# Routing a mixture of experts in two parts: the first 48 token tiles inside the attention stage, the last 16 behind it

## The reference, cut to what matters

```python
x = x + ga * attention(layernorm(x) * (1 + ca) + sa)
h = layernorm(x) * (1 + cb) + sb
logits = einsum('bsh,eh->bse', h, router_w)           # 8 experts
probs = softmax(logits)
weights, indices = top_k(probs, 2)
weights = weights / (weights.sum(-1, keepdims=True) + 1e-06)
gate, up = split(einsum('bsh,ehi->bsei', h, w13))      # 2 x 512 per expert
y = einsum('bsei,eih->bseh', silu(gate) * up, w2)
x = x + gb * (take(y, indices) * weights[..., None]).sum(2)
```

## Time and profile before

| what | us |
|---|---|
| median of 3 runs | 1350.82 |
| the three runs | 1350.82, 1351.5, 1343.63 |
| time of the profiled execution | 1345.89 |
| its span in the trace | 1344.1 |
| last logits copied by ACT | 677.96 |
| first instruction of the experts block | 678.23 |
| first gather on POOL | 723.14 |

### The profile page before, as it was taken

The page is one execution under the profiler, slowest core; times in us unless marked ns, Lnnn a source line. Parts: engine busy times, 40 slices in busy tenths (PEclk is TensorE's granted clock), DMA queues, the critical chain, the costliest instruction groups (busy, mean ns, idle before and its releaser), DMA issues. The chain is left out here.

```text
span 1344.1 us, 54731 instructions
## 1 busy us (share of the span) xinstructions
PE 1188.2 (88%) x20142; PEld 1014.1 (75%) x20142; DVE 939.0 (70%) x2509; ACT 706.3 (53%) x1391; POOL 929.5 (69%) x989
## 2 busy tenths in 40 slices
PE   3589999999899899998616899999999999999995
PEld 0377878778777777777405799999999999999994
DVE  2389999999999999988477555555555555555552
ACT  3277888888888888887531223322232223222221
POOL 3158999999999889998803466666666666666643
PEclk8599999999999999999555999999999999999998
DMA  9811333334333333343372354545454555555540
GB/s 232 173 54 49 84 97 91 88 102 119 106 102 115 96 111 105 104 116 108 92 201 72 72 96 94 98 93 96 90 97 94 96 97 98 98 99 97 97 70 1
DMA packets 126348, 134.52 MB, mean 100 GB/s; under 512 B 26298, under 2 KB 104210, under 8 KB 125970
## 3 DMA queue, kind: packets, MB, share of 16 engines
q0 software_dynamic: 32592, 56.75, 21.9%
q1 hardware_dynamic: 89762, 67.46, 18.8%
q10 hardware_dynamic: 3744, 6.82, 1.8%
HBM read 63.58 MB, written 44.04 MB: 80 GB/s over the span
## 5 line engine op out<-in xcount | busy, mean ns | idle before, releaser
L1143 PE MATMUL psum<-xT,xall 128*128 128x256 f16 x3408 | 397.2, 274 | 1.5 <-DVE xT L1130 0.9
L1203 POOL DMA_INDIRECT out<-yo,sidx x142 | 226.5, 1595 | 198.9 <-DVE yo L1194 175.3
L1143 PEld LDWEIGHTS psum<-xT,xall 128*128 x3408 | 331.6, 98 | 40.0 <-issue 1.9
L1151 ACT ACTIVATE sg<-psum 128x512 f32<-128x512 f32 x142 | 84.7, 597 | 318.7 <-PE psum L1143 304.6
L1156 DVE SCALAR_TENSOR_TENSOR hf<-psum,sg 128x512 f32<-128x512 f32 x142 | 98.3, 692 | 214.4 <-ACT sg L1151 208.3
L1113 POOL DMA_INDIRECT grow<-moe_rows,gidx x142 | 144.4, 1017 | 93.7 <-DVE sidx L1001 50.8
L1177 PE MATMUL psum<-w2s,hT 128*128 x1704 | 199.3, 274 | 3.8 <-DVE w2s L1229 3.5
L1177 PEld LDWEIGHTS psum<-w2s,hT 128*128 128x128 f16 x1704 | 167.4, 98 | 24.4 <-issue 4.3
L1163 ACT ACTIVATE hT<-hf 128x512 f16<-128x512 f32 x142 | 89.4, 630 | 112.7 <-DVE hf L1156 100.6
L569 POOL TENSOR_TENSOR pT<-sc,pT 128x1024 f16<-128x1024 f32 x64 | 136.7, 2135 | 9.8 <-ACT pT L565 9.8
L1167 DVE TENSOR_TENSOR hT<-hf,hT 128x512 f16<-128x512 f32 x142 | 98.4, 693 | 57.0 <-ACT hT L1163 49.4
(11 more groups left out here) (217 smaller groups left out, 2414.1 us busy)
## 6 DMA issues: line engine op xcount, KB each, us to landing
stk<-qk SPq DMA_DIRECT2D x384, 64.0 KB, 2.8
moe_rows<-hrows SPq DMA_DIRECT2D x128, 128.0 KB, 2.7
out<-xall SPq DMA_DIRECT2D x128, 64.0 KB, 2.4
xall<-in_x SPq DMA_DIRECT2D x8, 896.0 KB, 17.6
raw<-in_w ACTq DMA_DIRECT2D x26, 256.0 KB, 3.2
raw<-in_w SPq DMA_DIRECT2D x8, 512.0 KB, 8.8
grow<-moe_rows,gidx POOLq DMA_INDIRECT x142
out<-yo,sidx POOLq DMA_INDIRECT x142
```

Of the source, the lines that this page charges most:

```text
L1143: i = k.e.matmul(bank[:, n * LONG:(n + 1) * LONG], w13s[:, bass.ds(ex_reg * (G * 4 * I) + ((2 * c + b_) * 2 * I + col), P)], xT[:, k.b, a, ...
L1151: done(k.e.activation(sg[:, half, :], bGate[half][:, :], ACT.Silu, scale=1.0 / W_SCALE), "sg")
L1203: k.e.indirect_dma_start(out_rows, bass.IndirectOffsetOnAxis(ap=sidx[:, n:n + 1], axis=0), yo[:, k.v, q, :], None, bounds_check=B * T - 1, ...
```

## The change

The chain over 64 tiles becomes a class `Part` with methods for its steps, made twice: `early` for tiles 0 to 47 (384 elements in a partition) and `late` for tiles 48 to 63 (128 elements).

- Early on DVE, in rounds 73 to 76: the choice of the best two, 12 instructions and the one that makes `chosen`, behind `ln2_shift` (`choice_a`), `resid` (`choice_b`) and `var_eps2` (`choice_c`). Behind DVE's rounds, still in the attention block: `early_rest`, with the weights, the count and the places.
- Early on ACT: two Exp behind `logit_copy` of round 75. On PE: two prefix matmuls behind `router` of round 71 into banks B and C.
- Early on SP: behind its last `store`, 8 transfers with the weights of 12 of the 16 segments, and behind the waits for the stores a wait for these 8 to have landed.
- In the experts block the chain runs over 16 tiles; one subtraction more takes the counts of the early part into account, and `tile_0` is made by two instructions. Eight transfers write the remaining weights. From `rsel` on all is as before.
- The early scratch lies in buffers of the attention that are free by then (`ex`, `rel`, `sig`, `qk`), what the late part needs in `wqkv`, which now lives through both blocks. `hf` and `yo` of the slots lie on `late13`.

```diff
+EARLY = 48
+N_EARLY = E * EARLY
+ROUND_CHOICE, ROUND_PREFIX, ROUND_EXP = 73, 71, 75
...
+    def gaps2(self, e, s_gap):
+        e.tensor_tensor(self.e2, self.m2, self.m1, ALU.subtract).then_inc(s_gap, 1)
+        self.link(e, e.tensor_tensor(self.gap2, self.gap2, bc_mid(self.m2, E), ALU.subtract))
...
+        start = upto[:, :, 0]
+        if self.t0:
+            self.link(e, e.tensor_tensor(self.start, start, self.placed.cnt, ALU.subtract))
...
+    def choice_a(e, i):
+
+        if i == ROUND_CHOICE:
+            e.wait_ge(S["lg"], EARLY)
+            early.largest(e)
+            early.gaps(e, e_gap)
+        if i == ROUND_CHOICE + 1:
+            early.one_hot(e, early.oh1, early.r1)
+        if i == ROUND_CHOICE + 2:
+            early.gaps2(e, e_gap)
+        if i == ROUND_CHOICE + 3:
+            early.one_hot(e, early.oh2, early.r2)
+            early.choose(e, e_chosen)
+    def choice_b(e, i):
+
+        if i == ROUND_CHOICE + 1:
+            early.without_first(e)
+        if i == ROUND_CHOICE + 2:
+            early.hits(e, early.gap2)
+    def choice_c(e, i):
+
+        raw_low(e, i)
+        if i == ROUND_CHOICE:
+            early.hits(e, early.gap)
+            early.first_of(e, early.r1)
+        if i == ROUND_CHOICE + 1:
+            early.second(e)
+        if i == ROUND_CHOICE + 2:
+            early.first_of(e, early.r2)
...
+        if i == ROUND_EXP:
+            e.wait_ge(e_gap, 2)
+            e.activation(early.ex, early.gap, ACT.Exp).then_inc(e_exp, 1)
+            e.activation(early.e2, early.e2, ACT.Exp).then_inc(e_exp, 1)
+    def early_prefix(e, i):
+        if i == ROUND_PREFIX:
+            e.wait_ge(S["umul"], NT)
+            e.wait_ge(e_chosen, 1)
+            for q, bank in enumerate((bkB, bkC)):
+                e.matmul(bank[:, 0:N_EARLY], trib[:, q, :], chosen.bitcast(BF16), start=True, stop=True).then_inc(e_prefix, 1)
+    def early_rest(e):
+        e.memset(one, 1.0)
+        e.memset(early.seen[:, 0:1], 0.0)
+        early.weights(e, e_exp, e_chosen, e_placed)
+        e.wait_ge(e_prefix, 2)
+        early.count(e, one, by_expert(bkB[:, 0:N_EARLY]), bkC[:, 0:N_EARLY], placed.cnt)
+        early.place(e, e_placed)
+    chunk_work = {p_high: raw_load, logit_copy: early_exp, ln2_shift: choice_a, resid: choice_b, var_eps2: choice_c,
+                  router: early_prefix}
...
             engine_program("sync", e)
+            e.wait_ge(e_placed, 1)
+            weights_out(e, rows_dram, early.w8, 0, EARLY // NJ, e_w8)
             for j in range(4):
                 e.wait_ge(s_st[j], 32 * NS)
             for j in range(4):
                 e.wait_ge(s_out[j], 32 * NS)
+            e.wait_ge(e_w8, 16 * B)
...
             engine_program("vector", e)
+            early_rest(e)
```

More of the change, by code:

```diff
@@ L49 @@
 OOB = B * T + 4096
+NGATHER, NADD = 6, 4
 NCH, NEARLY, NRAW = E * G, 13, 3
@@ L80, in adaln_block @@
         passed = sem("passed")
+        s_g, s_sc = [sem(f"f_row{i}") for i in range(NGATHER)], [sem(f"f_add{i}") for i in range(NADD)]
         idf = sb("idf", [P, P])
@@ L814, in raw_low, with taken, by_expert @@
             w13_low(e, w13s, raw[:, n % NRAW, :], n).then_inc(s_rlo, 1)
-    chunk_work = {p_high: raw_load, logit_copy: raw_high, var_eps2: raw_low}
+    e_v, e_gap, e_exp, e_chosen = sem("e_v"), sem("e_gap"), sem("e_exp"), sem("e_chosen")
+    e_prefix, e_placed, e_w8 = sem("e_prefix"), sem("e_placed"), sem("e_w8")
+    def taken(home, *sizes):
+        at = [sum(sizes[:i]) for i in range(len(sizes) + 1)]
+        return [home[:, a:b] for a, b in zip(at, at[1:])]
+    def by_expert(ap):
+        return ap.rearrange("p (e t) -> p e t", e=E)
@@ new lines, in attention @@
+    NE = N_EARLY
+    gap, gap2, m1, m2, e2, z, g = taken(ex[:, :, :].rearrange("p b n -> p (b n)"), NE, NE, *([EARLY] * 5))
+    expd, seen, one, oh1 = taken(rel[:, :, :].rearrange("p b n -> p (b n)"), NE, NE + 1, 1, NE // 2)
+    where, w8, hit = taken(sig[:, :, :, :, :, :].rearrange("p k a g b t -> p (k a g b t)"), NE, NE, NE // 2)
+    oh2, chosen, over, row_at, r1, r2, row32 = taken(qk[:, :, :, :, :].rearrange("p b w a n -> p (b w a n)"), NE, NE, NE, NE,
+                                                     EARLY, EARLY, 4 * EARLY)
@@ new lines, in attention @@
+    early = Part(0, EARLY, dict(
+        gap=by_expert(gap), gap2=by_expert(gap2), m1=m1, m2=m2, e2=e2, z=z, g=g, ex=by_expert(expd), seen=seen,
+        oh1=by_expert(oh1.bitcast(F16)), where=by_expert(where), w8=w8.rearrange("p (t e) -> p t e", e=E),
+        hit=by_expert(hit.bitcast(F16)), oh2=by_expert(oh2), chosen=by_expert(chosen.bitcast(BF16)), over=by_expert(over),
+        row_at=by_expert(row_at), r1=r1, r2=r2, row32=row32.bitcast(F32).rearrange("p (t q) -> p t q", q=2)),
+        placed, placed.lt0, logits, iota, tok_id, e_v)
@@ L906, in route_sync @@
         e.wait_ge(s_weights, 1)
[L907 to L912, removed]
+        weights_out(e, rows_dram, w8, EARLY // NJ, NS, s_w8)
     def route_vector(e):
         def link(ins):
[L915 to L920, removed]
+            late.link(e, ins)
         e.memset(one[:, :], 1.0)
@@ L971, in route_vector @@
-        link(e.tensor_copy(row_of[:, :, :], row32[:, :, :]))
+        late.largest(e)
+        late.gaps(e, s_gap)
+        late.hits(e, late.gap)
+        late.first_of(e, late.r1)
+        late.one_hot(e, late.oh1, late.r1)
+        late.without_first(e)
+        late.second(e)
+        late.gaps2(e, s_gap)
+        late.hits(e, late.gap2)
+        late.first_of(e, late.r2)
+        late.one_hot(e, late.oh2, late.r2)
+        late.choose(e, s_chosen)
+        late.weights(e, s_exp, s_chosen, s_weights)
@@ L972, in route_vector @@
+        e.wait_ge(s_prefix, 2)
+        late.count(e, one, bBefore[:, 0:E * NL].rearrange("p (e t) -> p e t", e=E), bTotal[:, 0:E * NL], cnt[:, :])
+        late.place(e, s_asel)
         groups = 2 * NT // NHOT
-        rows = row_of[:, :, :].rearrange("p t q -> p (t q)")
+        rows = row_of.rearrange("p t q -> p (t q)")
         for k in range(groups):
@@ L1016, in route_scalar @@
         e.wait_ge(s_gap, 2)
[L1017 to L1018 removed]
+        e.activation(late.ex, late.gap, ACT.Exp).then_inc(s_exp, 1)
+        e.activation(late.e2, late.e2, ACT.Exp).then_inc(s_exp, 1)
         e.wait_ge(s_2, 16 * E)
```

182 lines of the change are left out of this document (108 added, 74 removed).

## The result

| | before | after |
|---|---|---|
| median of 17 runs each, us | 1348.53 | 1354.33 |
| lowest to highest | 1342.91 to 1353.36 | 1347.93 to 1360.36 |
| span of the profiled execution | 1344.1 | 1358.2 |

The account below looks back on a forecast made before the run. PE bounds attention and slots; the routing between is serial, so the first gather's shift decides. The block ends 6.8 us later, tile_no and gather 5.3: 1351.2 on the profiled execution, 1356.1 on the median, middle 1354; range 1347 to 1361.

Parts of the forecast that it names:

- path B: Loads of w2 after the experts block's start, eight ACT conversions, then tile_no: tile_no and first gather 5.3 us later.
- signs by which the forecast was to be wrong: Block end before 680 or after 690, tile_no waiting for DVE as before, or slots not taking 621 us.
- Step 1: DVE's late chain from z to first rsel: 15.25 us becomes 8.1, removing 7.2 us of this path.
- Step 2: DVE's choice instructions in rounds 73 to 76: all that follows comes 1.05 us later, bounds 0 and 7.2.
- Step 3: Exp on ACT and prefix matmuls on PE: 0.35 and 0.2 us on the last logits, covered by later steps.
- Step 4: DVE's early_rest behind its rounds: 12.8 us, ending at 683.2; alone it delays the attention block's end by 5.0.
- Step 5: SP's eight early weight writes and their landing end the attention block at 685.0, 6.8 us later than before.
- R1: Writes cost less, early_rest sets the block's end (+5.0), gather moves 3.5 us: 1349.4; chance 0.20.
- Step 6: Sum at the first gather: first rsel 0.4 us earlier, but tile_no and the gather 5.3 us later.
- R2: Each of 13 choice instructions delays its round, itself or through POOL: up to 7.2 us, 1357.3; chance 0.15.
- R3: Early part vanishes beside the last tiles, block ends as before; gain held to 1.5 us, 1344.4; chance 0.08.
- R4: Late chain isn't shortened because small instructions cost as much as large ones: +6.8, 1352.7; chance 0.02.

Follow-up runs that it names:

- after_tile_first: Changed kernel with ACT's eight w2 conversions moved behind tile_no and the two table copies; ln2_shift of tile 59 to first gather 77.5 us, ratio to before 0.9997.
- after_padded: Changed kernel with early f16 scratch hit at 64 elements per expert (stride 128 bytes, not 96); ln2_shift to first gather 83.6 us, one execution, no ratio.
- after_choice_behind: Changed kernel with all 13 choice instructions moved from DVE's rounds to the head of early_rest, Exp and prefix behind the rounds; ln2_shift to first gather 90.8 us.
- after_no_w8_wait: Changed kernel with the wait for the eight early weight writes moved from SP to POOL's first gather; ln2_shift to first gather 84.7 us, ratio to before 1.0082.
- split_tile_first: Changed kernel with early places in the experts block, early writes behind w2 loads, tile_no before w2 conversions; ln2_shift to first gather 72.0 us, ratio to before 0.9967.
- split: split_tile_first with tile_no back behind ACT's w2 conversions; ln2_shift of tile 59 to first gather 79.9 us, ratio to before 1.0024.

## Why the prediction was right, step by step

The forecast was 5.3 us more, and 1354 us. The mechanism on which it hangs was right: path B, the loads of w2 behind the block's end and the conversions ahead of tile_no, which after_tile_first shows. That the median came within 0.3 us of 1354 is luck in two ways. The middle between a quick execution and the median of three was chosen for want of a better one, and 17 runs put the median of before just there (1348.53). And the block's end came out near its forecast although another engine set it: a landing put too long was made up for by DVE's instructions, which were put too short in steps 2 and 4.

Two of the signs by which the forecast was to be wrong need a word. The block ended at 690.5, past the named 690, but this trace runs 4.55 us late before the change begins; on the scale of the kernel before it ended at 686.0. And the slots took 623.9 us in this trace for the 621 named; that is the part left open below.

- **Step 1, the late chain:** 8.1 us forecast, 7.4 measured from z to rsel. The first rsel was forecast at 57.7 on the scale above and came there, since the chain began 0.6 us later than forecast: two errors that cancel.
- **Step 2, the rounds:** 1.05 us forecast, 1.8 measured for gat of tile 62 and 1.9 for ln2_shift of tile 63. The term was mis-sized. The place was right in the main (rounds 74 and 75), but gap2 took 1.11 us for 0.56, and nmr of tile 61 slipped 0.8 for 0.45. Of this 0.8, 0.56 was already there at stats2 of tile 61 (11.45 us behind ln2_shift of tile 59 for 10.89), since POOL, beside the new L110 and L112, took 0.5 us more for two instructions (0.91 and 1.04 for 0.74 each) and so finished `res_add` late. `without_first` (L112) has no term in the sum at all: it cost DVE idle time alone, but it held POOL up. What I had put at 0, DVE and POOL holding each other up, was there: L106 took 1.87 us at 653.78, beside an instruction of 2.1 us on POOL, and 0.55 us at 666.18. The rule of the Trainium skill (GPSIMD Engine Reference, Key points: DVE instructions with two SBUF inputs contend with POOL) was the better guide than my 0; the traces agree with it, with 1.04 us for L127 beside POOL and 0.56 with POOL silent. That section gives no price: the 0.5 us for each of nine instructions were mine, with no row behind them, and the 4.5 us were not reached.
- **Step 3, Exp and prefix:** 0.55 us forecast (0.35 and 0.2), about 0.05 measured (6.46 us at ln2_shift of tile 63 to 6.51 at the last logits, between the two traces). It was covered in any case.
- **Step 4, early_rest:** 12.8 us forecast, 14.3 measured. Of the 1.5 us, 0.6 is the stride (two reductions, after_padded), and 1.2 is POOL (after_choice_behind); without both it would be 12.5. DVE's rest also began 0.75 us later than forecast, by step 2.
- **Step 5, SP:** this step failed in its order. I had the landing of the writes end the block, with step 4 1.8 us ahead. (That lead was mis-added: 685.0 has the 0.3 us of the engines' meeting in it and 683.2 has not, so it was 1.5, and R1 should have been 3.8 us, not 3.5.) In fact SP was through 0.9 us ahead of DVE, since the writes landed in 2.4 us (median of the eight) for the 3.4 assumed, and step 4 ran longer. The prediction set the 2.0 us of the Trainium skill (DMA: Bandwidth & Descriptors, Anatomy of one DMA) beside this; that section gives its figure for transfers issued by GpSimd, these are issued by SP, and the shortest of them took 2.3. The end came out at 40.6 for 39.7: R1's mechanism (DVE's rest ends the block) with nearly the forecast's size. after_no_w8_wait shows that the landing cost nothing.
- **Step 6, the sum:** path B was the mechanism, and it is the part on which sign and size hang. 5.3 us forecast, 6.6 measured in the stretch and 5.8 by the medians; after_tile_first takes the loss away whole by ACT's order alone. The 1.3 us between 5.3 and 6.6 are 0.9 for the block's later end and 0.6 for w2, whose first conversion began 19.0 us behind the first load for 18.4 before, less 0.2 between tile_no and gather.
- **The rivals:** R2 (gaps are not gaps) was right in kind and small: 1.8 us, not 7.2. R3 (the early part vanishes beside the last tiles) is what split_tile_first comes near to, by moving the places out of the block, and its bound of 1.5 us of gain holds only while ACT keeps its order: split_tile_first won 5.8 in the stretch. R4 is out by step 1. The "another 3.5 us" for the upper price of step 5 should have been 4.4 (12.5 for 8.1); nothing hung on it.

What stays open: the 2.9 us more from first gather to the end in the profiled execution. In the other traces this part takes 619.6 to 624.0 us, and the values don't follow the edits. PE's clock differs there. Clock and DMA in the windows behind the first gather, of the changed kernel (us, busy of PE, PEld, DVE, ACT, POOL, granted clock, DMA share, GB/s):

```profile
745.00:750.00 5.00, 5.00 (x46) 4.23 (x44) 2.90 (x4) 1.23 (x2) 3.78 (x5) 0.87 0.61 178
750.00:755.00 5.00, 3.37 (x32) 2.49 (x31) 0.69 (x1) 1.12 (x2) 1.55 (x2) 1.00 0.59 174
755.00:760.00 5.00, 2.40 (x22) 1.91 (x20) 4.83 (x7) 0.59 (x2) 0.00 (x0) 1.00 0.00 1
760.00:765.00 5.00, 4.09 (x20) 2.96 (x21) 3.84 (x6) 1.75 (x3) 0.00 (x0) 0.50 0.00 0
765.00:770.00 5.00, 5.00 (x43) 4.18 (x42) 1.29 (x5) 0.60 (x1) 1.70 (x2) 0.82 0.02 3
770.00:775.00 5.00, 5.00 (x48) 4.48 (x46) 3.22 (x6) 1.85 (x3) 3.47 (x3) 1.00 0.72 111
```

The clock is granted in full (2.4 GHz), falls to half (1.2 GHz) behind five us of which PE was busy for 2.4, and then comes back. In the kernel before, 745 to 750, with PE busy for 1.8 of five us, it was granted at 0.84, at 0.82 in the next five, and in no window between 735 and 775 at half throughout. How much of the 2.9 us this makes wasn't tried, so its cause stays open.

## What to carry to other kernels

When a serial chain is shortened by moving half of it ahead of a barrier, ask what else starts at that barrier: here the loads behind it moved with the barrier, and a queue that was in a harmless order for 1.5 us of slack then set the end. Three things belong together: move the work, keep what is moved from ending the block later, and reorder the queue whose work would then end last. Moved work and the new order alone only broke even (after_tile_first, 77.5 for 77.8), moved work and the earlier block end alone lost 2.1 us (split), and all three gave 5.8 us in the stretch. Fixed landmarks on both sides of the changed stretch showed differences of 1 us where the whole time scatters by 10.

## What I had not expected of the hardware

- A reduction over experts of 384 f16 elements took 1.10 us with a stride of 96 bytes, more than 512 elements with a stride of 128 bytes (1.04 us in the kernel before, L967), and 0.80 us once padded to 128. With f32 elements and a stride of 192 bytes it took 0.78 to 0.81.
- DVE and POOL instructions that overlap did not both slow down a little: in the rows above the one begun second ended late, behind the other. Small DVE instructions were stretched too (48 elements in 0.51 us for 0.21), among them one with a single input tensor (L125, 0.63 us for 0.19), while the reduction L123 took 0.80 us beside POOL and with POOL silent. And POOL's instructions took 1.05 us beside DVE's new ones for 0.73 elsewhere (L776 at 651.04, L839 at 655.19), so the hold goes both ways.
